# Graph kernel on one core: in the first gather pass VectorE sums the four relations' count blocks and TensorE multiplies the sum once

## The reference: what is computed

```
h   = x @ W                                   # layer 0
out = segment_sum(h[src] * norm[:, None], dst)    # norm = deg^-1/2 at both ends
x   = layernorm(x + out)

for l in range(4):                            # layers with relations
    h   = einsum('ni,rio->rno', X, weights[l])
    agg = segment_sum(h[etype, src] * inv_deg[:, None], dst)
    X   = X + elu(layernorm(agg + X @ roots[l] + biases[l]) * gamma + beta)
x   = layernorm(x + X)
```

## Time and profile before

| | |
|---|---|
| time, median of 3 runs | 4994.74 us (4990.61 to 4995.69) |
| time of the profiled execution | 4996.72 us |
| its span, first to last instruction | 4994.8 us |
| TensorE busy | 4517.6 us, 90% of the span |
| VectorE busy | 3576.0 us, 72% |
| GpSimd busy | 3114.7 us, 62% |
| ScalarE busy | 1408.2 us, 28% |
| mean granted clock of TensorE | 0.963 of full speed |

### The profile page before, as it was taken

How to read it: one execution, slowest core, us unless ns; L and a number is a source line. 1 busy time by engine, 2 the same in 40 slices (tenths; PEclk the granted TensorE clock), 3 DMA queues, 4 the chain that set the end, 5 groups by cost and what they waited for, 6 DMA issues and landing times.

```text
span 4994.8 us, 79070 instructions
## 1 busy us (share of the span) xinstructions
PE 4517.6 (90%) x20583; PEld 3371.0 (67%) x20583; DVE 3576.0 (72%) x9682; ACT 1408.2 (28%) x3565; POOL 3114.7 (62%) x3096
## 2 busy tenths in 40 slices
PE   6688888477899999899999899999899999899997
PEld 5444444234788877688887688887688887677775
DVE  7998888689677777566666566666566666577776
ACT  1016665441565664112112111211111211111111
POOL 0028887200677775777775677775677775677775
PEclk9899999689999999999999899999899999899998
DMA  2000000751666666766666666666666666666565
GB/s 58 1 1 1 1 1 2 270 204 60 183 197 195 199 192 170 240 196 197 193 193 165 213 197 195 192 195 168 205 197 193 195 194 172 191 182 181 179 180 148
DMA packets 411454, 786.55 MB, mean 157 GB/s; under 512 B 76847, under 2 KB 167809, under 8 KB 411000
## 3 DMA queue, kind: packets, MB, share of 16 engines
q0 software_dynamic: 143040, 365.21, 28.5%
q1 hardware_dynamic: 266936, 415.27, 24.7%
q10 hardware_dynamic: 1152, 2.10, 0.1%
HBM read 666.07 MB, written 115.89 MB: 157 GB/s over the span
## 4 chain that ended last, share of the span: by engine, by line
PE 71%; DVE 12%; issue 6%; DMA 4%; POOL 3%; DVEq 1%; ACT 1%; SPq 1%; ACTq 0%
PE psum L740 32%; PE psum L763 22%; PE psum L694 7%; POOL msg L588 2%; PE psum L798 2%; DVE arena L1227 2%; DVE arena L1289 2%; DMA msg<-h_table,g_rel 2%; DVE arena L1276 2%; PE psum L704 2%; PE psum L833 1%; PE psum L707 1%; DMA count_blocks<-emat 1%; DVE found L1362 1%; PE psum L626 1%
## 5 line engine op out<-in xcount | busy, mean ns | idle before, releaser
L588 POOL DMA_INDIRECT msg<-h_table,g_rel x1776 | 1694.7, 954 | 693.3 <-issue 343.2
L1416 DVE TENSOR_TENSOR arena<-arena,psum 128x256 f32 x2780 | 1155.4, 416 | 709.0 <-PE psum L763 679.7
L763 PE MATMUL psum<-msg,emat 128*128 128x256 f32 x4448 | 1312.6, 387 | 85.4 <-DMA msg<-h_table,g_rel 42.9
L763 PEld LDWEIGHTS psum<-msg,emat 128*128 128x128 f32 x4448 | 843.5, 193 | 363.5 <-issue 209.7
L1395 DVE TENSOR_SCALAR emat<-iota,node,weight 128x128 f32<-128x128 f32 x2224 | 808.2, 365 | 120.9 <-issue 32.2
L740 PE MATMUL psum<-arena,emat 128*128 128x256 f32 x3200 | 835.5, 385 | 19.2 <-issue 19.2
L588 POOL DMA_INDIRECT msg<-h_table,g_src x448 | 437.9, 977 | 490.1 <-PE psum L763 394.5
L570 POOL DMA_INDIRECT placed_rows<-leaving,idx x300 | 439.8, 1466 | 423.2 <-issue 419.1
L740 PEld LDWEIGHTS psum<-arena,emat 128*128 128x128 f32 x3200 | 607.5, 192 | 128.2 <-issue 46.9
L588 POOL DMA_INDIRECT hout<-h_table,g_rel x448 | 427.6, 954 | 184.2 <-issue 88.7
L798 PE MATMUL psum<-arena,emat 125*128 125x453 f16 x2000 | 447.8, 358 | 83.7 <-DVE arena L1289 83.7
(11 more groups left out here) (250 smaller groups left out, 5530.0 us busy)
## 6 DMA issues: line engine op xcount, KB each, us to landing
emat<-count_blocks SPq DMA_DIRECT2D x496, 256.0 KB, 3.3
more_blocks<-count_blocks SPq DMA_DIRECT2D x496, 256.0 KB, 3.4
count_blocks<-emat SPq DMA_DIRECT2D x200, 256.0 KB, 2.3
h_table<-hout SPq DMA_DIRECT2D x100, 512.0 KB, 3.3
msg<-h_table,g_rel POOLq DMA_INDIRECT x1776, 3.5
arena<-h_table SPq DMA_DIRECT2D x24, 512.0 KB
msg<-h_table,g_src POOLq DMA_INDIRECT x448, 3.6
hout<-h_table,g_rel POOLq DMA_INDIRECT x448, 3.4
```

Source lines behind the costliest of these rows:

```text
L588: pool.indirect_dma_start(out=slots[n % RING], out_offset=None, in_=table[:, :], in_offset=bass.IndirectOffsetOnAxis(ap=rows[:, t:t + 1], ...
L763: pe.matmul(agg_ps[n % NPS], emat[:, n % BODY, :], slots[n % RING], start=True, stop=True).then_inc(s_mm, 1)
L1416: dve.tensor_tensor(a, a, agg_ps[n % NPS], ALU.add).then_inc(s_acc, 1)
```

## The change

In pass 0 VectorE sums each block's four relations into one 128x128 block (a `tensor_reduce` over a view that takes the four values of a source and destination, 128 elements apart) in one of six buffers `rel_sums` in a part of `h_more` that pass 0 does not use. It does so SUM_AHEAD = 8 tiles ahead of the tile at which the block's first product stood; the sum waits for the block and for a free buffer, and it counts `s_used`. TensorE multiplies the sum with `hcache0[c]` once, where the block's first product stood, and counts a new semaphore `s_summed`. `dense_added` waits for that one in pass 0. Passes 1 to 4 keep their work.

```diff
+    SUM_AHEAD = 8
...
+        rel_sums = [h_more[:, 1 + k // 2, k % 2 * P:(k % 2 + 1) * P] for k in range(2 * (R - 1))]
...
+        s_summed = sem("s_summed")
...
-                if r == 0:
-                    pe.wait_ge(s_counts[c], (n + 1) * 16)
-                if q:
+                if q == 0:
+                    pe.wait_ge(s_used, n * K + c + 1)
+                    pe.matmul(dense_ps[0][:, 0:D], rel_sums[(n * K + c) % len(rel_sums)], hcache0[c],
+                              start=(c == 0), stop=(c == K - 1)).then_inc(s_summed, 1)
+                else:
+                    if r == 0:
+                        pe.wait_ge(s_counts[c], (n + 1) * 16)
                     to, first = dense_ps[r // 2][:, r % 2 * D:(r % 2 + 1) * D], r % 2 == 0
                     last = r % 2 == 1
-                    rows = hcaches[c][:, r, :]
-                else:
-                    to, first, rows = dense_ps[0][:, 0:D], r == 0, hcache0[c]
-                    last = r == R - 1
-                mm = pe.matmul(to, blocks[c][:, r * P:(r + 1) * P], rows,
-                               start=(c == 0 and first), stop=(c == K - 1 and last))
-                if r == R - 1:
-                    mm.then_inc(s_used, 1)
+                    mm = pe.matmul(to, blocks[c][:, r * P:(r + 1) * P], hcaches[c][:, r, :],
+                                   start=(c == 0 and first), stop=(c == K - 1 and last))
+                    if r == R - 1:
+                        mm.then_inc(s_used, 1)
...
-                    for i in range(K * R):
+                    for i in range(0, K * R, 1 if q else R):
                         put(work, dense_tile(j, i), lambda j=j, i=i: dense_product(q, j, i))
...
+            def relations_summed(j, c):
+                m = j * K + c
+                dve.wait_ge(s_counts[c], (j + 1) * 16)
+                if m >= len(rel_sums):
+                    dve.wait_ge(s_summed, m - len(rel_sums) + 1)
+                dve.tensor_reduce(rel_sums[m % len(rel_sums)],
+                                  blocks[c].rearrange("p (r d) -> p d r", r=R),
+                                  AXX, ALU.add).then_inc(s_used, 1)
+
             def add_tiles(q, work):
+                sums_at = {}
+                if q == 0:
+                    for j in range(NW):
+                        for c in range(K):
+                            put(sums_at, dense_tile(j, c * R) - SUM_AHEAD,
+                                lambda j=j, c=c: relations_summed(j, c))
                 for t in range(NT):
                     n = q * NT + t
+                    run(sums_at, t)
...
-                dve.wait_ge(s_used, (n + 1) * K)
+                dve.wait_ge(s_used if q else s_summed, (n + 1) * K)
```

## The result

The changed kernel takes 5049.7 us (median of 4, 5047.3 to 5052.6) against 4995.2 for the kernel before. The ratio is 1.0111 with a 95% interval of 1.0099 to 1.0123: slower by about 1.1%, clear of the 0.2% that can be told from no change. The forecast was 4988 in a range of 4970 to 5030, so the time lies outside.

What follows compares the result with a forecast made beforehand. TensorE was taken to bound the first gather pass, then VectorE: 634 us of own work + 80 for sums + 4 for waits gives 718 in place of 724.8, so 4994.7 - 7 gives 4988 us, range 4970 to 5030.

Steps and rivals of the forecast that it cites:

- The bound and the relief: First gather pass: TensorE bounds it; a faster TensorE gives back 92.4 us, then VectorE's 634 us bounds.
- 4 by choice: First pass: 4 us put on VectorE for TensorE's wait once a window for the normalised rows, from nothing to 8.
- The price of a sum: VectorE's 200 tensor_reduce in the first pass: 0.687 us each, of which 0.37 shows, 0.61 for one a window.
- The term of 80 us: What the sums add to VectorE's first pass: 3.2 us a window; bounds 58 and 168.
- The row of 223 ns: Trace of the kernel before: sum of four, 100 elements at 100 bytes, read as showing that a stride costs nothing extra.
- The stride as a rival: Slower: reading at 512 bytes doubles time per element; a sum takes 1.23 us, pass 91 more, 5086; chance 0.06.
- The drain as cover: A sum starts about 0.33 us after the tile's add ahead, so 0.32 of its 0.687 us does not show.
- The first rival, no cover: Slower: sums find no drain to lie in, each costs 0.61, pass 756, 31 us more, 5026; chance 0.17.
- The added waits at nothing: VectorE's sums waiting for count blocks and free buffers cost nothing; if either cover is gone, 24 us.
- GpSimd as the floor: Faster: sums cost 0.33, gathers set the pace, 12.5 to 28 us less, 20 taken: 4975; chance 0.10.
- TensorE's clock: Slower: at a mean granted clock of 0.59 the pass takes 768, 43 more, 5038; from 0.63 no cost; chance 0.05.
- a margin of 0.45 us a sum: Turning point for the first pass: 92.4 - 2 over 200 sums; a higher shown cost makes the change slower.

Runs made afterwards that it cites:

- the small add: Against the changed kernel: each sum made in two in-order adds, 128x256, then 128x128 in place a tile later (this one), five buffers; 4973.9 us, 0.9960.
- three buffers: Against the changed kernel: VectorE adds relations 0 and 1 to 2 and 3 in order, TensorE makes two products a chunk; 4978.1 us, 0.9968.
- the relief alone: Against the kernel before: one product a chunk in pass 0, of the first relation's block, and no sums; 4964.9 us, 0.9949.

## Why the prediction was wrong, step by step

- **The bound and the relief: right.** VectorE took over. Of its 105.3 us of waits for TensorE, 13.2 are left. The forecast had 2 at the start and 4 by choice. It put VectorE's own work 6 us too high, at 632 for 626, because it took off a wait for the add ahead in 42 places where no add stands directly ahead.
- **The price of a sum: wrong, and alone enough.** The step that failed is the term "so 512 take 806 - 113 x 1.05 = 687 ns", and the sentence behind it, that the one sum with a stride took "not more than the plain 256". The term of 80 us measured 143, and the prediction's own sign of it, sums over 1 us, came. With reads in order a sum was what the step said: 676 ns, and 69 us for the 200 against 80. That the pass of that run, 718.4, meets the forecast is luck, for the gathers set it. The row of 223 ns was one value at another place than the rows beside it: it had begun under the instruction ahead of it. By one row of a size, start-up and slope can't be told apart; the second size (500 values) shows the double slope.
- **The stride as a rival: right mechanism, chance and price too low and too high.** It got 0.06 against that row, though the prediction itself named a rule that spoke for it. Its price of 91 us came from the doubled slope with the whole start-up (1.23 us a sum, 0.91 shown). Measured were 1.05 and 0.72.
- **The drain as cover: right.** Sums start 0.34 us behind the add; 0.32 of each lies in time that VectorE had lost anyway. The rule that the next operation starts only when the pipe has emptied (the Trainium skill, VectorE: DVE Perf Modes, "The DRAIN you can't avoid") would have made the small add cost its 0.28; it cost nothing. The same section adds that an operation that is not held starts earlier, which the prediction left out, and the rows show such a start: the small add began 0.33 us after an add of 0.42. The first rival, no cover, is out.
- **The added waits at nothing: right** for the blocks and for the six buffers: no wait of a sum stands in the changed kernel's list of VectorE's waits. With three buffers such waits came, and cost little.
- **GpSimd as the floor: right for the relief, too low with sums.** 12.5 to 28 us less was the bound; the relief alone gave 25.5. But that GpSimd's 684 "do not cut in" would have failed even at the price that the forecast gave the sums: with sums in order the gathers took 704.6 us and set the pace.
- **TensorE's clock: little cost at most.** It fell to 0.87, and all of VectorE's waits for products, whatever their cause, come to 10.8 us. TensorE's work was put too low: 553 us busy in place of 453. Most of that is not the clock, for the relief alone gives 544 at 0.96. The 0.63 from which the clock would have decided was worked out from the 453.
- **The sign of the whole** hung on a margin of 0.45 us a sum with a price read at 0.37. That margin was thin beside the one row that carried it, and the range to 5030 did not cover the stride.

## What to carry to other kernels

When work moves from the busiest engine to the next one, price it from a row with the same access pattern and the same predecessor: an instruction that starts under the one ahead of it can be recorded shorter (222 ns against 325), and a step through memory can double the time per value (2.02 ns against 1.05 at 100 bytes). Where a sum over a few blocks is needed, adds of neighbouring columns beat one reduction across them (0.42 and 0.28 us against 1.05), and placed between an operation and the one that waits for it they can be free. And look for the third engine: here 259 us less on TensorE are worth 25, because the gathers' issue is next.

## What the hardware showed beyond that

- A sum of 512 f32 values takes 0.69 us in order or at 8 bytes, 1.00 to 1.07 at steps of 16 to 512 bytes, and 0.69 again for pairs at 1 KB. Why pairs are free stays open.
- Gathers are longer in the runs with sums: 0.974 us on the mean with no sums, 0.991 to 1.011 in the runs with added sums that read in order, where the gathers' issue sets the pass. It happens with adds of two inputs and with reductions of one. The median stays at 0.946 to 0.949; what grows is the number of gathers over 1.1 us, from 35 of 505 with no sums to 80 of 494 with the reductions in order. In that run the gathers that overlap a sum are not the longer ones (0.990 us on the mean, the others 1.027). What lengthens the few stays open.
